# Layernorm and gate of a two-layer network in one block, with the scaling on GpSimd and the spills inside the first attention

## The chip, the cores and the metric

The kernel is written for one Trainium2 chip and runs on 1 of its cores. The metric is the device time of one launch in microseconds (us), shorter is better. Engines are named as the profile names them: PE is TensorE, DVE is VectorE, ACT is ScalarE, POOL is GpSimd, and SP is the sync engine, which issues most of the DMAs.

## The reference

Only the first parts of the first layer touch the change. The input `x` has 8 batches of 512 rows and 256 features.

```python
h = (x - mean(x)) / sqrt(var(x) + 1e-5)          # layernorm over the 256 features
attn = attention(h, W_qkv, W_out)                # 16 key/value heads, 32 query heads, alibi slopes, causal
logits = mean(h, axis=1) @ w_gate + b_gate       # one row of 8 logits a batch
probs = softmax(logits); top_vals, top_idx = top_k(probs, 2)
gate_w = top_vals / sum(top_vals)
a = clip(alpha, 0.1, 1.0)
ffn = a * main(h) + (1 - a) * sum(gate_w[k] * expert[top_idx[k]](h) for k in (0, 1))
x1 = x + silu(ffn) * attn
```

The second layer (a recurrence, a second attention, routing and experts) follows, and the change does not touch it.

## The kernel before

The program is a row of phases. Each opens a block in which every engine has its own instruction stream, and at a block's end all engines meet at a barrier. The first three phases are `layernorm_phase`, `gate_phase` and `head_attention_phase`; then comes `network_phase`, the first reader of the spilled halves and of the gate's results.

`layernorm_phase` makes one pass a batch. SP loads a batch of 512 KB into one of two buffers `x_in`. DVE takes the statistics (`bn_stats`, L113, and `bn_aggr`, L117), ACT the root (L144), and DVE the reciprocal (L119) and the scaling of the batch in place, four instructions of 128x256 (L122). PE transposes it by eight products with the identity (L166) into one of two pairs of PSUM banks. ACT copies each bank into `xh`, rounded to the form in which PE multiplies, and sums the columns into `xsum` (L153). DVE writes the remainder, bank less `xh`, into `xl` (L134). SP stores both halves, 512 KB each, to DRAM (L92, L93).

The loops run over pairs of batches. DVE's order is: all of pass n + 1 up to its scaling, then the remainder of batch n. SP's order is: wait for the transposes of batch n, load batch n + 2, wait for its remainder, store both halves. So a load stands behind the two stores of the batch before it. Loads and passes wrap around: ten loads are issued and DVE and ACT make nine passes, the last of them on a second copy of the first batch, since the loop has no special case for its end. The block ends only when the last store has landed (L96).

`gate_phase` loads the gate's weights, multiplies `xsum` by them on PE (L226), and runs some twelve tiny instructions on DVE, each waiting for the one before (`link`), with one `Exp` on ACT (L232). Beside them GpSimd clears the accumulator `acc` in one instruction (L219). SP then writes two tiny tables to DRAM, `rows` (which expert's weights to load) and `coef` (their factors), waits for both, reads them back in the layout that the network needs (L209 to L213), and waits again before the block ends.

`head_attention_phase` runs 16 heads of 8 batches. SP loads a head's weights (L674, L675, later L696 and L698) and copies each batch's keys `k_parts` within SBUF into two partition halves, `k_twice` (L681). At the start GpSimd splits the first head's weights (L714, L716), and PE's first product waits for that. GpSimd also scales the probabilities in every step (L723).

```python
sp.wait_ge(turned, (pair * 2 + par) + 1)                        # L84
sp.dma_start(x_in[par][:], ...)
sp.wait_ge(low, (pair * 2 + par) + 1)                           # L90
sp.dma_start(xh_dram[...], xh[...]); sp.dma_start(xl_dram[...], xl[...])
```

## Time and profile before

| quantity | value |
|---|---|
| three runs | 3632.81, 3629.51, 3629.32 us |
| their median | 3629.51 us |
| the profiled execution's own time | 3632.09 us |
| its span, first to last instruction | 3630.3 us |
| outside the span (3632.09 less 3630.3) | 1.8 us |
| PE busy over the span | 3332.2 us, 92% |
| DVE, ACT, POOL busy | 68%, 60%, 32% |
| mean granted clock of TensorE | 0.961 |
| from the start to the gate's first instruction | 62.0 us |
| from the gate's first instruction to the attention's first | 13.3 us |
| from the attention's first instruction to PE's first product | 7.9 us |

The profiled execution lies within the three runs, near the slower of them. A share of busy time over the whole span is a mean over stages with different limits: PE is 92% busy in all and almost idle in the first 83 us, which is the stretch that the change rewrites. So the stages are read one by one.

### The profile page before, as it was taken

How to read it: one execution, taken by the hardware profiler on the slowest of the kernel's cores; microseconds unless marked ns; L12 is line 12 of the kernel's file. 1: busy time of each engine (PE TensorE's matmuls, PEld its weight loads, DVE VectorE, ACT ScalarE, POOL GpSimd, SP SyncE). 2: the span in 40 equal slices, each digit the busy share in tenths (PEclk: the TensorE clock that was granted, in tenths of full speed). 3: DMA queues.
4: the chain of work that ended last, by engine and by line, in shares of the span. 5: the costliest groups of instructions: out<-in, count | busy, mean ns of one | idle time of the engine just before them, and what ended most of it. 6: DMA issues, size and time to landing. Idle time of an engine off the chain costs nothing. (4 is left out here: it accounts for less than half of the span.)

```text
span 3630.3 us, 67556 instructions
## 1 busy us (share of the span) xinstructions
PE 3332.2 (92%) x19106; PEld 2540.4 (70%) x19106; DVE 2452.3 (68%) x7032; ACT 2169.8 (60%) x5052; POOL 1178.1 (32%) x1802
## 2 busy tenths in 40 slices
PE   2999999999999999997999997979999965999995
PEld 1777777777777777776888885546666654788885
DVE  5777777777777777776666664546666635666665
ACT  1777777777777777775565554215565640555553
POOL 1333333333333333334333331022313102244442
PEclk9999999999999999999999998978999976999998
DMA  4222222222222222224333432110111123554545
GB/s 163 44 51 45 50 46 47 49 45 51 45 51 45 47 44 49 47 46 154 117 127 127 135 116 96 53 49 22 30 27 30 27 80 110 153 142 122 142 123 156
DMA packets 176586, 281.45 MB, mean 78 GB/s; under 512 B 32466, under 2 KB 118226, under 8 KB 176466
## 3 DMA queue, kind: packets, MB, share of 16 engines
q1 hardware_dynamic: 161874, 259.98, 24.8%
q0 software_dynamic: 14592, 19.93, 3.4%
q8 instruction: 67, 1.10, 0.1%
q14 instruction: 53, 0.43, 0.0%
HBM read 160.84 MB, written 41.16 MB: 56 GB/s over the span
## 5 line engine op out<-in xcount | busy, mean ns | idle before, releaser
L723 POOL TENSOR_SCALAR at_p<-at_p,at_recip 128x128 f32<-128x128 f32 (+3 forms) x1028 | 537.0, 535 | 981.2 <-DVE at_recip L862 981.2
L773 ACT ACTIVATE at_p<-at_p,at_nmax 128x128 f32<-128x128 f32 (+3 forms) x1030 | 575.6, 559 | 291.1 <-DVE at_nmax L856 287.9
L856 DVE CUSTOM_DVE_ANT_0 at_p<-at_s_ps,at_bias 128x128 f32<-128x128 f32 (+3 forms) x1030 | 493.6, 479 | 155.8 <-PE at_s_ps L971 155.8
L978 PE MATMUL at_t_ps<-ident,at_p 128*128 128x128 f32 x2560 | 460.0, 278 | 0.1
L970 PE MATMUL at_s_ps<-at_k_twice,at_q 128*128 128x128 f32 (+3 forms) x1030 | 388.4, 377 | 8.0 <-DVE at_nmax L856 1.2
L1795 DVE CUSTOM_DVE_ANT_0 aa_a_ps<-aa_a_ps,aa_hidden 128x128 f32<-128x128 f32 (+3 forms) x512 | 247.3, 507 | 173.8 <-PE aa_a_ps L1959 170.7
L971 PE MATMUL at_s_ps<-at_k_twice,at_q 128*128 128x128 f32 (+3 forms) x1030 | 332.9, 323 | 0.0
L978 PEld LDWEIGHTS at_t_ps<-ident,at_p 128*128 128x128 f32 x2560 | 294.9, 140 | 46.3 <-DVE at_pT L869 29.9
L988 PE MATMUL at_o_ps<-at_pT,at_v 128*64 128x512 f32 (+3 forms) x2064 | 306.8, 439 | 0.0
L1695 ACT ACTIVATE aa_pT<-aa_b_ps 128x512 f32<-128x512 f32 (+1 forms) x384 | 196.6, 529 | 176.0 <-PE aa_b_ps L1977 173.2
L988 PEld LDWEIGHTS at_o_ps<-at_pT,at_v 128*64 128x64 f32 x2064 | 136.8, 137 | 176.4 <-issue 157.3
L438 ACT ACTIVATE nw_h<-nw_h_ps,nw_b 128x512 f32<-128x512 f32 x192 | 132.2, 689 | 211.8 <-PE nw_h_ps L535 211.4
L970 PEld LDWEIGHTS at_s_ps<-at_k_twice,at_q 128*128 128x128 f32 x1030 | 194.7, 189 | 91.1 <-DVE at_nmax L856 44.6
L869 DVE COPY at_pT<-at_t_ps 128x128 f32<-128x128 f32 (+3 forms) x512 | 238.9, 467 | 0.0
L508 DVE SCALAR_TENSOR_TENSOR nw_hl<-nw_h,nw_coef_now,nw_hh 128x512 fp32r<-128x512 f32 x192 | 154.8, 806 | 115.3 <-ACT nw_hh L443 115.3
L2510 POOL DMA_INDIRECT moe_dram<-ex_o,places x76 | 124.9, 1643 | 302.9 <-ACT ex_o L2537 211.8
L781 ACT ACTIVATE at_pT<-at_t_ps 128x128 f32<-128x128 f32 (+3 forms) x512 | 218.9, 428 | 6.2
L391 POOL TENSOR_SCALAR nw_w1h<-nw_w_raw 128x256 fp32r<-128x256 f32 x200 | 106.7, 533 | 337.5 <-PE nw_o_ps L546 317.2
L843 DVE TENSOR_TENSOR at_k_parts<-at_m_ps,at_k_parts 64x512 fp32r<-64x512 f32 x130 | 88.8, 683 | 179.5 <-ACT at_vT L767 179.5
L1959 PE MATMUL aa_a_ps<-aa_k,aa_q 128*128 128x128 f32 (+3 forms) x512 | 191.3, 386 | 14.8 <-DVE aa_nmax L1795 11.7
L971 PEld LDWEIGHTS at_s_ps<-at_k_twice,at_q 128*128 128x128 f32 x1030 | 196.6, 191 | 11.4
L933 PE MATMUL at_m_ps<-xh,at_wh 128*128 128x512 f32 (+1 forms) x520 | 185.2, 437 | 20.7 <-POOL at_wl L716 18.6
(315 smaller groups left out, 8467.3 us busy)
## 6 DMA issues: line engine op xcount, KB each, us to landing
at_k_twice<-at_k_parts SPq DMA_DIRECT2D x260, 256.0 KB, 3.3
nw_w_raw<-in_w_all_dram SPq DMA_DIRECT2D x52, 1024.0 KB, 7.4
w_raw<-in_w_dram SPq DMA_DIRECT2D x57, 768.0 KB
ln_x<-in_x_dram SPq DMA_DIRECT2D x10, 512.0 KB, 4.8
nw_xh<-xh_dram SPq DMA_DIRECT2D x10, 512.0 KB, 4.4
nw_xl<-xl_dram SPq DMA_DIRECT2D x10, 512.0 KB, 4.9
at_w_raw<-in_w_heads_dram SPq DMA_DIRECT2D x18, 256.0 KB, 3.4
nw_x<-in_x_dram SPq DMA_DIRECT2D x9, 512.0 KB, 7.0
```

The source lines that it names most:

```text
L723: pool.tensor_scalar(p, p, recip[:, u:u + 1], 1.0, ALU.mult, ALU.mult).then_inc(scaled, 1)
L773: act.activation(p_sb[:, u, 0:N], p_sb[:, u, 0:N], ACT.Exp, bias=nmax[:, u:u + 1], scale=-1.0, accum_out=total[:, u:u + 1]).then_inc(exped, 1)
L781: act.activation(pT[par][:, 1, 0:qt + 1, qt * P:N], t_ps[1][:, 0:N].rearrange("p (k q) -> p k q", q=P), ACT.Copy).then_inc(odd_out, 1)
L856: dve.tensor_tensor_reduce(out=p_sb[:, u, 0:N], in0=s_ps[u % 2][:, 0:N], in1=bias[:, u % 2, S - N:S], scale=1.0, scalar=BIG, op0=ALU.add, ...
L869: dve.tensor_copy(pT[par][:, 0, 0:qt + 1, qt * P:N], t_ps[0][:, 0:N].rearrange("p (k q) -> p k q", q=P))\
L970: pe.matmul(s_ps[u % 2][:, 0:N], q, k_twice[par][:, 0, 0:N], start=True, stop=False)
L971: pe.matmul(s_ps[u % 2][:, 0:N], q, k_twice[par][:, 1, 0:N], start=False, stop=True).then_inc(scored, 1)
L978: ins = pe.transpose(t_ps[u % 2][:, k * P:k * P + P], p_sb[:, u, k * P:k * P + P], ident[:])
L988: ins = pe.matmul(o_ps[HD * h:HD * h + HD, k * P:S], v[par][:, k, :], pT[par][:, h, k, k * P:S], start=(k == 0), stop=(k == TT - 1))
L1695: act.activation(pT[group_of(n, s) % 2][:, s % REP, piece * S:piece * S + N], b_ps[done % 3][:, 0:N], ACT.Exp, scale=-1.0)\
L1795: dve.tensor_tensor_reduce(out=a_ps[i % 2][:, 0:N], in0=a_ps[i % 2][:, 0:N], in1=hidden[:, S - N:S], scale=1.0, scalar=BIG, op0=ALU.add, o ...
L1959: pe.matmul(a_ps[i % 2][:, 0:N], q_all[n % 2][:, head // 2, N - P:N], k_all[n % 2][:, head % 2, g, 0:N], start=True, stop=True).then_inc(s ...
```

## The change

There are five edits.

1. The layernorm's loops are written out for 8 batches. There are three buffers `x_in` and three pairs of PSUM banks in place of two, and two sets of `mv` and `rstd`. Exactly eight loads and eight passes are made. DVE's order becomes: reciprocal of n + 1, statistics of n + 2, remainder of n.
2. The scaling is done by GpSimd, four instructions a batch. After each batch's scaling GpSimd clears an eighth of `acc`.
3. The gate is the last part of the layernorm's block, with no barrier ahead of it. Its weights are loaded behind the first three batches. The last remainder stands between its first steps and the rest.
4. The stores of `xh` and `xl` are taken out of the layernorm's block. SP issues one at the end of each head of the attention, `xh` of a batch after an even head and `xl` of it after an odd one: 16 in all.
5. The gate's round trip through DRAM is moved into the attention's SP stream: the writes before the first copies of the keys, the reads after them. The waits for its end and for the stores stand at the end of that block.

POOL, at the start of the program. Before (`ident` is the identity, `acc` the accumulator, `at_rel` the attention's first tile):

```order
L102 AFFINE_SELECT ident<-ident 128x128
L53 UNCONDITIONAL_BRANCH
L217 UNCONDITIONAL_BRANCH
L219 MEMSET acc 128x8192
L181 UNCONDITIONAL_BRANCH
L704 UNCONDITIONAL_BRANCH
```

And with the change:

```order
L116 AFFINE_SELECT ident<-ident 128x128
L122 TENSOR_SCALAR ln_x<-ln_x,ln_mv,ln_rstd 128x256 x4
L124 MEMSET acc 128x2x512
L122 TENSOR_SCALAR ln_x<-ln_x,ln_mv,ln_rstd 128x256 x4
L124 MEMSET acc 128x2x512
L122 TENSOR_SCALAR ln_x<-ln_x,ln_mv,ln_rstd 128x256 x4
```

The pair of rows comes eight times. GpSimd had nothing to do in the layernorm, and now stands between DVE's reciprocal and PE's transposes of every batch; the one long clearing is cut into eight.

DVE, one batch in the middle of the layernorm and the passage into the gate. Before:

```order
L113 BN_STATS ln_stats<-ln_x 128x6 x4
L114 ISA
L115 MEMSET ln_carry 128x1
L117 BN_AGGR ln_mv<-ln_stats 128x2 x4
L118 REGISTER_ALU
L119 RECIPROCAL ln_rstd<-ln_std 128x4
L122 TENSOR_SCALAR ln_x<-ln_x,ln_mv,ln_rstd 128x256 x4
```

With the change, the last batches and the gate's beginning:

```order
L144 RECIPROCAL ln_rstd<-ln_std 128x4
L135 BN_STATS ln_stats<-ln_x 128x6 x4
L140 BN_AGGR ln_mv<-ln_stats 128x2 x4
L150 TENSOR_TENSOR xl<-ln_ps,xh 128x512 x2
L144 RECIPROCAL ln_rstd<-ln_std 128x4
L150 TENSOR_TENSOR xl<-ln_ps,xh 128x512 x2
L172 MEMSET row_sb 8x1
L175 SCALAR_TENSOR_TENSOR gt_logits<-gt_ps,gt_bg 8x8
L177 TENSOR_REDUCE gt_tiny<-gt_logits 8x1
L150 TENSOR_TENSOR xl<-ln_ps,xh 128x512 x2
L180 RECIPROCAL gt_tiny<-gt_tiny 8x1
L181 TENSOR_SCALAR gt_logits<-gt_logits,gt_tiny 8x8
```

The four scalings have left DVE, the reciprocal comes before the next batch's statistics, and the last remainder lies between the gate's second step and its third.

SP, from the attention's start into its loop. Before, the row of `at_k_twice` came right behind that of `at_wo_raw`. With the change:

```order
L648 DMA at_wo_raw<-in_wo_heads_dram 128x256
L657 DMA rows_dram<-row_sb 8x3
L658 DMA coef_dram<-coef_sb 8x3
L654 DMA at_k_twice<-at_k_parts 64x1024 x4
L662 DMA rows<-rows_dram 1x24
L663 DMA coef<-coef_dram 128x24
```

And at the end of an even head:

```order
L673 DMA xh_dram<-xh 256x1x512
L675 ISA
L677 ISA
L677 DMA at_w_raw<-in_w_heads_dram 128x512
L679 ISA
L679 DMA at_wo_raw<-in_wo_heads_dram 128x256
```

The store stands ahead of the loads of a later head's weights, behind all copies of keys of its own head.

The diff without the declarations and without the removed lines, which the listing above shows.

```diff
@@ -48,19 +48,35 @@
...
+    XR = 3
...
+        x_in = [sb(f"ln_x{i}", [P, TT, D]) for i in range(XR)]
...
+        mv = [sb(f"ln_mv{i}", [P, TT, 2]) for i in range(2)]
...
+        rstd = [sb(f"ln_rstd{i}", [P, TT]) for i in range(2)]
...
+        xT_ps = [[ps(f"ln_ps{i}{k}") for k in range(KT)] for i in range(3)]
...
+        x_loaded = [sem(f"ln_x_loaded{i}") for i in range(XR)]
...
@@ -68,32 +84,30 @@
...
         @block.sync
         def _(sp):
...
+            for n in range(B):
+                if n >= XR:
+                    sp.wait_ge(turned, n - XR + 1)
+                sp.dma_start(x_in[n % XR][:], x_view[n]).then_inc(x_loaded[n % XR], 16)
+                if n == XR - 1:
+                    sp.dma_start(wg[:], w_gate.rearrange("(k p) e -> p k e", p=P)).then_inc(loaded, 16)
+                    sp.dma_start(bg[:], b_gate.rearrange("(a e) -> a e", a=1).broadcast_to([B, E0])).then_inc(loaded, 16)
+                    sp.dma_start(al[:], alpha.broadcast_to([B, 1])).then_inc(loaded, 16)
+            sp.wait_ge(loaded, 48)
+            for i in range(XR):
+                sp.wait_ge(x_loaded[i], 16 * len(range(i, B, XR)))
         @block.gpsimd
         def _(pool):
@@ -101,139 +115,42 @@
...
+            for n in range(B):
+                pool.wait_ge(rstd_done, n + 1)
+                for i in range(TT):
+                    pool.tensor_scalar(x_in[n % XR][:, i, :], x_in[n % XR][:, i, :], mv[n % 2][:, i, 0:1],
+                                       rstd[n % 2][:, i:i + 1], ALU.subtract, ALU.mult).then_inc(normed, 1)
+                pool.memset(acc[:, :, n * S:n * S + S], 0.0).then_inc(cleared, 1)
+            pool.wait_ge(cleared, B)
         @block.vector
         def _(dve):
             dve.memset(eps[:], EPS_LN).then_inc(eps_done, 1)
...
+            def spread(n):
+                dve.wait_ge(x_loaded[n % XR], 16 * (n // XR) + 16)
                 for i in range(TT):
...
+                    dve.bn_stats(stats[:, i, :], x_in[n % XR][:, i, :]).then_inc(stats_done, 1)
                 dve.wait_ge(stats_done, n * TT + TT)
...
+                if n >= 2:
+                    dve.wait_ge(normed, (n - 1) * TT)
                 for i in range(TT):
...
+                    dve.bn_aggr(mv[n % 2][:, i, :], stats[:, i, :]).then_inc(var_done, 1)
+            def invert(n):
                 dve.wait_ge(std_done, n + 1)
...
+                dve.reciprocal(rstd[n % 2][:], std[:]).then_inc(rstd_done, 1)
+            def remainder(n):
+                for k in range(KT):
+                    dve.wait_ge(high, n * KT + k + 1)
+                    ins = dve.tensor_tensor(xl[:, k, n * S:n * S + S], xT_ps[n % 3][k][:],
+                                            xh[:, k, n * S:n * S + S].bitcast(F32), ALU.subtract)
+                ins.then_inc(low, 1)
...
@@ -242,11 +159,23 @@
...
+            spread(0)
+            invert(0)
+            spread(1)
+            for n in range(B):
+                if n + 1 < B:
+                    invert(n + 1)
+                if n + 2 < B:
+                    spread(n + 2)
+                if n < B - 1:
+                    remainder(n)
+            dve.memset(row_sb[:, 0:1], 0)
             dve.wait_ge(ready, 1)
             link(dve.scalar_tensor_tensor(out=logits[:], in0=l_ps[0:B, 0:E0], scalar=1.0 / S, in1=bg[:],
                                           op0=ALU.mult, op1=ALU.add))
             link(dve.tensor_reduce(tiny[:, 0:1], logits[:], AX.X, ALU.max, negate=True))
+            remainder(B - 1)
             dve.wait_ge(exped, 1)
             link(dve.reciprocal(tiny[:, 2:3], tiny[:, 1:2]))
             link(dve.tensor_scalar(logits[:], logits[:], tiny[:, 2:3], None, ALU.mult))
@@ -258,8 +187,48 @@
             link(dve.tensor_scalar(coef_sb[:, 0:1], al[:], 0.1, 1.0, ALU.max, ALU.min))
             link(dve.tensor_scalar(tiny[:, 5:6], coef_sb[:, 0:1], -1.0, 1.0, ALU.mult, ALU.add))
             link(dve.tensor_scalar(coef_sb[:, 1:NF], top[:, 0:TOP], tiny[:, 4:5], tiny[:, 5:6], ALU.mult, ALU.mult))
...
             link(dve.tensor_scalar(row_sb[:, 1:NF], at[:, 0:TOP], 1.0, None, ALU.add))
+        @block.scalar
+        def _(act):
+            act.wait_ge(eps_done, 1)
+            def root(n):
+                act.wait_ge(var_done, n * TT + TT)
+                if n >= 1:
+                    act.wait_ge(rstd_done, n)
+                act.activation(std[:], mv[n % 2][:, :, 1], ACT.Sqrt, bias=eps[:, 0:1]).then_inc(std_done, 1)
+            root(0)
+            root(1)
+            for n in range(B):
+                act.wait_ge(turned, n + 1)
+                for k in range(KT):
+                    act.activation(xh[:, k, n * S:n * S + S], xT_ps[n % 3][k][:], ACT.Copy,
+                                   accum_out=xsum[:, k, n:n + 1]).then_inc(high, 1)
+                if n + 2 < B:
+                    root(n + 2)
+            act.wait_ge(chain, 2)
+            act.activation(logits[:], logits[:], ACT.Exp, bias=tiny[:, 0:1], accum_out=tiny[:, 1:2])\
+                .then_inc(exped, 1)
+        @block.tensor
+        def _(pe):
+            pe.wait_ge(id_done, 2)
+            for n in range(B):
+                pe.wait_ge(normed, n * TT + TT)
+                if n >= 3:
+                    pe.wait_ge(low, n - 2)
+                for k in range(KT):
+                    for i in range(TT):
+                        ins = pe.transpose(xT_ps[n % 3][k][:, P * i:P * i + P], x_in[n % XR][:, i, P * k:P * k + P], ident[:])
+                ins.then_inc(turned, 1)
+            pe.wait_ge(loaded, 48)
+            pe.wait_ge(high, B * KT)
+            for k in range(KT):
+                ins = pe.matmul(l_ps[0:B, 0:E0], xsum[:, k, :], wg[:, k, :], start=(k == 0), stop=(k == KT - 1))
+            ins.then_inc(ready, 1)
...
@@ -573,7 +542,8 @@
...
+def head_attention_phase(nc, w_heads, wo_heads, slopes, ident, xh, xl, acc, xh_dram, xl_dram, row_sb, coef_sb,
...
@@ -613,6 +583,9 @@
...
@@ -681,8 +654,14 @@
...
+            sp.dma_start(rows_dram, row_sb[:]).then_inc(gate_out, 16)
+            sp.dma_start(coef_dram, coef_sb[:]).then_inc(gate_out, 16)
             copy_k(1, 0)
             copy_k(4, 1)
+            sp.wait_ge(gate_out, 32)
+            sp.dma_start(rows[:], rows_dram.rearrange("(a b) f -> a (b f)", a=1)).then_inc(gate_back, 16)
+            sp.dma_start(coef[:], coef_dram.rearrange("(a b) f -> a (b f)", a=1).broadcast_to([P, B * NF]))\
+                .then_inc(gate_back, 16)
             with sp.Fori(0, KVH // 2) as jj:
                 for jp in range(2):
                     j = jj * 2 + jp
@@ -690,6 +669,8 @@
                         for par in range(2):
                             copy_k(kv_count(j * B + pair * 2 + (par + 2)), par)
+                    to, half = ((xh_dram, xh), (xl_dram, xl))[jp]
+                    sp.dma_start(to[:, :, ds(jj * S, S)], half[:, :, ds(jj * S, S)].bitcast(F32)).then_inc(spilled, 16)
                     sp.wait_ge(w_split, j + 1)
                     sp.wait_ge(wo_split, j + 1)
@@ -697,6 +678,8 @@
                         .then_inc(w_loaded[jp], 16)
                     sp.dma_start(wo_raw[jp][:], wo_heads[ds((j + 2) % KVH, 1)].rearrange("a p n -> p (a n)"))\
                         .then_inc(w_loaded[jp], 16)
+            sp.wait_ge(gate_back, 32)
+            sp.wait_ge(spilled, 32 * B)
             for i in range(2):
                 sp.wait_ge(w_loaded[i], 32 * (KVH // 2 + 1))
                 sp.wait_ge(k_copied[i], 32 * (KVH * B // 2 + 1))
@@ -2694,14 +2677,16 @@
...
+                layernorm_phase(nc, x, ident, xh, xl, xsum, acc, w_gate, b_gate, alpha, row_sb, coef_sb, spent)
+                head_attention_phase(nc, w_heads, wo_heads, slopes, ident, xh, xl, acc, xh_dram, xl_dram, row_sb, coef_sb,
+                                     rows_dram, coef_dram, rows, coef, spent)
...
                           spent)
...
```

## Rows read from the trace of the kernel before

**Rows 1.** by stage: us; busy PE, PEld, DVE, ACT, POOL; clock, DMA, GB/s

```profile
0.00:62.00 62.00, 15.75 (x64) 12.55 (x64) 39.60 (x143) 13.30 (x42) 0.68 (x6) 1.00 0.66 220
62.00:75.40 13.40, 0.26 (x4) 0.15 (x4) 5.20 (x14) 1.68 (x3) 6.92 (x1) 1.00 0.02 2
...
83.10:100.00 16.90, 13.59 (x42) 9.81 (x42) 5.70 (x19) 6.30 (x17) 0.05 (x1) 0.88 0.29 62
100.00:1600.00 1500.00, 1493.36 (x9106) 1105.23 (x9106) 1181.11 (x3844) 1135.90 (x3078) 561.93 (x1050) 1.00 0.22 47
```

**Rows 2.** timeline, first batch: start, us, engine line op out<-in xcount

```profile
4.71 1.41 DVE L113 BATCH_NORM_STATS2 ln_stats<-ln_x 128x6 f32<-128x256 f32 x4 [3.79 <-DMA ln_x<-in_x_dram]
...
8.24 0.18 DVE L119 RECIPROCAL ln_rstd<-ln_std 128x4 f32<-128x4 f32 x1 [1.71 <-ACT ln_std L144]
...
9.89 1.97 PE L166 MATMUL ln_ps<-ident,ln_x 128*128 128x128 f32 x8 [9.89 <-DVE ln_x L122]
...
11.93 0.18 DVE L119 RECIPROCAL ln_rstd<-ln_std 128x4 f32<-128x4 f32 x1 [0.36 <-ACT ln_std L144]
...
12.60 0.59 ACT L153 ACTIVATE xh<-ln_ps 128x512 f32 x1
...
13.44 1.28 DVE L134 TENSOR_TENSOR xl<-ln_ps,xh 128x512 f32 x2
```

**Rows 3.** timeline, statistics of the third batch and of the ninth pass

```profile
15.78 1.40 DVE L113 BATCH_NORM_STATS2 ln_stats<-ln_x 128x6 f32<-128x256 f32 x4 [1.05 <-DMA ln_x<-in_x_dram]
...
51.80 1.41 DVE L113 BATCH_NORM_STATS2 ln_stats<-ln_x 128x6 f32<-128x256 f32 x4 [1.09 <-DMA ln_x<-in_x_dram]
```

**Rows 4.** timeline, the gate and the boundaries around it

```profile
62.03 6.92 POOL L219 MEMSET acc<- 128x8192 f32 x1 [60.52 <-POOLq L53]
...
64.75 0.15 DVE L249 TENSOR_REDUCE gt_tiny<-gt_logits 8x1 f32<-8x8 f32 x1
...
65.62 3.35 DVE L252 TENSOR_SCALAR gt_logits<-gt_logits,gt_tiny 8x8 f32<-8x8 f32 x1
...
70.50 0.15 DVE L262 TENSOR_SCALAR gt_row<-gt_at 8x2 uint32<-8x2 uint32 x1
...
75.53 0.58 DVE L818 CAST at_woh<-acc 128x256 fp32r<-128x256 f32 x1 [4.89 <-PEq L181]
```

**Rows 5.** POOL: one timeline row of the attention scaling; one group

```profile
1208.36 0.94 POOL L723 TENSOR_SCALAR at_p<-at_p,at_recip 128x256 f32<-128x256 f32 x2 [1.22 <-DVE at_recip L862]
...
L716 POOL TENSOR_TENSOR at_wol<-at_wo_raw,at_woh 128x256 fp32r<-128x256 f32 x16 | 11.8, 735 | 1.3
```

**Rows 6.** DMA issues: out<-in, engine, op, count, KB each, us to landing

```profile
at_k_twice<-at_k_parts SPq DMA_DIRECT2D x260, 256.0 KB, 3.3
...
ln_x<-in_x_dram SPq DMA_DIRECT2D x10, 512.0 KB, 4.8
...
xl_dram<-xl SPq DMA_DIRECT2D x8, 512.0 KB, 4.1
```

**Rows 7.** timeline of SP at the end of the first head

```profile
196.56 0.35 SPq L696 DMA_DIRECT2D at_w_raw<-in_w_heads_dram  x1
...
207.07 86.35 SPq L681 DMA_DIRECT2D at_k_twice<-at_k_parts  x16
```

**Rows 8.** timeline, a copy of k issued and the first read of it

```profile
1205.82 13.30 SPq L681 DMA_DIRECT2D at_k_twice<-at_k_parts  x4
...
1213.44 0.32 PE L970 MATMUL at_s_ps<-at_k_twice,at_q 128*128 128x128 f32 x1
```

**Rows 9.** waits of SP and timeline at the end of the attention

```profile
SPq L585 <- PEq L585: 8.3, 1, 8.3
...
1670.41 0.06 DVE L452 MEMSET nw_bsum<- 128x4 f32 x1 [0.36 <-PEq L585]
```

**Rows 10.** timeline, two of the first products of the attention, on PE

```profile
84.15 1.05 PE L933 MATMUL at_m_ps<-xh,at_wl 128*128 128x512 f32 x2
...
91.90 0.63 PE L933 MATMUL at_m_ps<-xh,at_wl 128*128 128x512 f32 x2
```

More of the change, by code:

```diff
@@ L73, in layernorm_phase @@
         low = sem("ln_low")
-        spilled = sem("ln_spilled")
+        loaded = sem("gt_loaded")
+        chain = sem("gt_chain")
+        exped = sem("gt_exped")
+        ready = sem("gt_ready")
         x_view = x_dram.rearrange("b (i p) d -> b p i d", p=P)
@@ L125, in _ @@
-            norm(0, 0, 0)
-            with dve.Fori(0, B // 2) as pair:
-                for par in range(2):
-                    n = pair * 2 + par
-                    norm(n + 1, pair + par, 1 - par)
-                    dve.wait_ge(high, n * KT + KT)
-                    at = n * S
-                    for k in range(KT):
-                        ins = dve.tensor_tensor(xl[:, k, ds(at, S)], xT_ps[par][k][:], xh[:, k, ds(at, S)].bitcast(F32),
-                                                ALU.subtract)
-                    ins.then_inc(low, 1)
@@ L138, in _ @@
-        @block.scalar
-        def _(act):
-            act.wait_ge(eps_done, 1)
-            def root(n):
-                act.wait_ge(var_done, n * TT + TT)
-                act.activation(std[:], mv[:, :, 1], ACT.Sqrt, bias=eps[:, 0:1]).then_inc(std_done, 1)
-            root(0)
-            with act.Fori(0, B // 2) as pair:
-                for par in range(2):
-                    n = pair * 2 + par
-                    root(n + 1)
-                    act.wait_ge(turned, n + 1)
-                    for k in range(KT):
-                        act.activation(xh[:, k, ds(n * S, S)], xT_ps[par][k][:], ACT.Copy,
-                                       accum_out=xsum[:, k, ds(n, 1)]).then_inc(high, 1)
@@ L156, in _ @@
-        @block.tensor
-        def _(pe):
-            pe.wait_ge(id_done, 2)
-            with pe.Fori(0, B // 2) as pair:
-                for par in range(2):
-                    n = pair * 2 + par
-                    pe.wait_ge(normed, n * TT + TT)
-                    for k in range(KT):
-                        for i in range(TT):
-                            ins = pe.transpose(xT_ps[par][k][:, P * i:P * i + P], x_in[par][:, i, P * k:P * k + P], ident[:])
-                    ins.then_inc(turned, 1)
@@ L573, in _ @@
             turn(B, 1)
-def head_attention_phase(nc, w_heads, wo_heads, slopes, ident, xh, xl, acc, spent):
+def head_attention_phase(nc, w_heads, wo_heads, slopes, ident, xh, xl, acc, xh_dram, xl_dram, row_sb, coef_sb,
+                         rows_dram, coef_dram, rows, coef, spent):
     with ExitStack() as ctx:
```

115 lines of the change are left out of this document (21 added, 94 removed).

## The prediction, made before the change was run

> **What bounds the kernel now.** I read the times by stage first [rows 1]. In the attention, from 100 to 1600 us, PE is busy for 1493.4 of 1500 us: nothing that leaves PE's work there alone can shorten it. In the first 62 us PE is busy for 15.8 us, and in the 13.4 us of the gate for 0.3. So the start is bound by chains of waits and the rest by PE. The change touches only the start, and moves some DMAs under the attention.
>
> Then the timeline of the layernorm [rows 2, 3]. The statistics of the third batch begin at 15.78 and those of the ninth pass at 51.80: six passes in 36.0 us, 6.0 a pass, and each waits about 1 us for the DMA of its batch. DMA runs at 220 GB/s there [rows 1]: a pass moves 1.5 MB, a load behind two stores, and the load lands 4.8 us after its issue in the median [rows 6]. After the ninth pass come the last stores, and the gate begins at 62.03.
>
> Last the gate [rows 4]. DVE's tiny instructions take 0.15 us each, save one of 3.35 us, which ends at 68.97, where GpSimd's clearing of `acc` ends too (62.03 plus 6.92 is 68.95). The nine after it end at 70.65, 0.19 each. Then comes the round trip through DRAM, and DVE's first instruction of the attention stands at 75.53, after 4.89 us of idle time.
>
> **The change, part by part.** All is measured up to that last point, DVE's first cast of the attention.
>
> *First batch.* The statistics begin at 4.71 as before and the reciprocal ends at 8.42 [rows 2]. Scaling is now GpSimd's. The trace has no such instruction (two scalars a row) on GpSimd; the nearest is the scaling of the probabilities, same size, one such scalar, two in 0.94 us, 0.47 each [rows 5]. The other end is GpSimd's instruction with two whole inputs of that size, 0.735 [rows 5]. I take 0.47, since only one tensor is read: 1.88 us a batch, against 1.4 on DVE. With the hand-offs the transposes start at 10.5 and, at 1.97 us [rows 2], end at 12.5.
>
> *Each further batch.* Three costs compete. DVE: statistics and their sum 1.82 (4.71 to 6.53, where the 1.71 us of idle time before the reciprocal begins), reciprocal 0.18, remainders 1.28 [rows 2], with gaps 3.5. GpSimd: 1.88 of scaling plus an eighth of 6.92 [rows 4], 0.87, so 2.75. One of three buffers round its loop: load 3.9 (DVE waited 3.79 us for the first), statistics 1.82, root and reciprocal 0.54 [rows 2], scaling 1.88, transposes 1.97, hand-offs 0.3: 10.4, a third of it 3.5. The first and the last are equal, and as DVE works in a fixed order each delays the other at times. Placing the eight batches one after another with these durations, each engine in its written order, I get the last transposes ending at 38.7: 26.2 us for seven batches, 3.75 each in place of 6.0. ACT's two copies, 0.59 each and a read of the sum behind each [rows 2], end at 40.1. The stores are no longer there to be waited for, and neither is the ninth pass. Against 62.0 that is 21.9 us less.
>
> *Gate.* Its weights landed long before. The product takes 0.3 with its hand-off (0.26 busy [rows 1]), DVE's first two steps 0.4, then the last remainder 1.28, which covers ACT's table load and `Exp`, then eleven steps at 0.19, 2.1: it ends at 44.2. The 3.35 us stall goes, as GpSimd's last clearing ends near 38. The round trip, most of the 4.89 us, leaves the path: the writes and reads are tiny and have the whole attention to land. A barrier costs 0.36 us where nothing else is late [rows 9]. DVE's first cast then stands at 44.6 instead of 75.53, 30.9 less. I take 30.5, for hand-offs that I cannot price.
>
> That stall is where the Trainium skill bears on this change. Taken by itself, the row says that a DVE instruction can stand still as long as a GpSimd instruction runs; were that so for the statistics, DVE's 3.5 and GpSimd's 2.75 would add, and that is a rival below. The Trainium skill (SBUF — State Buffer, "Who interferes with whom") says that the two share a pair of ports, an exclusive lock, which a DVE instruction wants only in a two-port mode or with two inputs in SBUF. By it neither the statistics (one input) nor the remainder (one input in PSUM) waits, and the time would be 3599.0 us, as below, and not the 3616.5 of the first reading. No row of this trace has the statistics beside GpSimd, so the row does not settle it.
>
> *Attention.* Its first 8 us are unchanged. Sixteen stores of 512 KB are added, 8.4 MB. Each is issued behind the copies of keys of its head. At a head's end the weights' load is issued at 196.56 and the next copy of keys at 207.07 [rows 7]; a store lands within 4.1 us [rows 6]. So it is gone before the next copy. A copy has cover of its own: issued at 1205.82, its second half 0.6 later, landing 3.3 us after that, and first read at 1213.44 [rows 8], 3.7 us to spare. The first weights are needed a head later. The gate's four DMAs stand where SP has nothing to issue but the next keys. I cost all of it at nothing; if the cover were gone it would be the 4.1 us of a store, sixteen times. At the end SP waited 8.3 us for the others at the barrier [rows 9]; the last store takes at most 0.6 plus 4.1 of that.
>
> **Sum.** 3632.1 less 30.5 is 3601.6 against the profiled execution. That execution lies 2.6 us above the median of the three runs; against the median I get **3599.0 us**.
>
> Bounds: with transposes at 1.2 us a batch (PE has two levels of speed, below) and a load in 3.3, the same placing gives 3.5 less. With GpSimd at 0.735 and loads at 4.8 it gives 5.6 more. The runs before spread over 3.5 us.
>
> **The rivals.**
>
> *A. GpSimd and DVE take turns* (8 in 100). For it: the row of 3.35 us. Against it: the reduction at 64.75, beside the same clearing, took its usual 0.15 [rows 4]. A batch would take 3.5 plus 2.75, 6.25 us, so 2.5 more for seven batches: 17.5 us, 3616.5 us.
>
> *B. PE reaches its upper level earlier* (8 in 100). In the first products of the attention a pair took 1.05 us at 84.15 and 0.63 at 91.90 [rows 10]; I read that as the lower level, 1.2 GHz, and the upper, 2.4 GHz, though the granted clock is 0.88 in the mean over that stretch [rows 1]. PE had been almost idle since the layernorm's last transposes. With the change it rests some 14 us between those, at 38.7, and its first product at 52.5. Six pairs came before the row at the upper level; were they at that level, each would save 0.42 us at most, and three more later if the clock held: nine pairs, 3.8 us, 3595.2 us.
>
> *C. The stores reach PE, and the kernel is slower* (3 in 100). The place is `k_twice`: SP's queue is served in order, so a store that still moves data when the next copy is issued delays it; PE has nothing else to do, being 99.6% busy. Each store would have to cost PE more than 30.5 over 16, 1.9 us, for a loss. If its full 4.1 us came through at each head it would be 65.6 us: 3664.6 us. Against it stand the 10.5 us between head's end and next copy.
>
> *D. The gain is given back* (3 in 100). The waits moved to the attention's end would have to end last there, beyond the 8.3 us of SP's waiting, or the layernorm's pass would have to stay at 6 us because of its loads. With both, the time would be within 7 us of the one before: 3627.
>
> **How the numbers follow.** My forecast has 78 in 100, and is the likeliest. The range goes from 3593 (3599.0 less the 3.5 of the lower bound and part of B's 3.8) to 3608 (the upper bound, 3604.6, and the spread of the runs). It holds the forecast and B, and leaves out A, C and D, 14 in 100, and some of the forecast's own error. A measurement of this kernel can tell 0.2%, 7.3 us, from no change. Faster by more than that are the forecast, A and B: 0.94. Within it is D: 0.03. Slower is C: 0.03.
>
> **What would show it right or wrong.** Right: GpSimd's scalings near 0.47 us each, statistics starting 3.5 to 4 us apart, DVE's statistics still 1.41 us for four, no DVE instruction of some us in the gate, DVE's first cast near 44.6, PE as busy in the attention as before, and no wait of PE for `k_twice`. Wrong: a scaling of 0.7 us or more, statistics stretched wherever GpSimd works (A), loads that land later than 4.8 us though no store is there, a row of PE waiting for the copies (C), or SP as the last engine at the attention's end (D).

## The result and the profile of the changed kernel

| | before | changed kernel |
|---|---|---|
| median of 7 runs, us | 3629.68 (3627.29 to 3633.75) | 3617.72 (3610.81 to 3620.19) |
| ratio, 95% interval | | 0.9961 (0.9951 to 0.9971) |
| profiled execution, us (its span) | 3632.09 (3630.3) | 3613.86 (3612.1) |
| mean granted clock | 0.961 | 0.962 |
| DVE's first cast of the attention, us | 75.53 | 61.41 |

The changed kernel is 0.39% faster: by the ratio 14.2 us of 3629.7, with an interval from 10.5 to 17.8; the two medians differ by 12.0. The forecast said 30.5 us and 3599.0 us, with a range up to 3608; the result lies 9.7 us above that range. The first cast of the attention moved by 14.12 us, which lies within the interval of the gain. So the search is for the 16.8 us that are missing ahead of one instruction (61.41 where 44.6 was forecast); the median is 18.7 us above the forecast, and the other 1.9 us are taken up at the end of the section on why the prediction was wrong.

First the page and the table by stage (start and end, length, then busy PE, PEld, DVE, ACT, POOL, granted clock, DMA share, GB/s), which answers to [rows 1].

```profile
PE 3329.0 (92%) x19106; PEld 2537.6 (70%) x19106; DVE 2434.8 (67%) x6978; ACT 2168.2 (60%) x5051; POOL 1212.5 (34%) x1841
```

```profile
0.00:56.70 56.70, 15.72 (x64) 12.55 (x64) 24.00 (x88) 13.17 (x42) 46.29 (x46) 1.00 0.23 74
56.70:61.20 4.50, 0.25 (x4) 0.17 (x4) 3.26 (x15) 1.61 (x3) 0.00 (x0) 1.00 0.00 0
69.00:100.00 31.00, 27.10 (x130) 19.33 (x132) 17.36 (x57) 18.51 (x49) 8.01 (x16) 0.94 0.25 52
100.00:1600.00 1500.00, 1493.36 (x9110) 1104.77 (x9106) 1181.37 (x3845) 1134.86 (x3077) 556.13 (x1044) 1.00 0.24 52
```

Three things stand there. The layernorm has lost its stores and its ninth pass: DMA runs at 74 GB/s where it ran at 220. DVE has lost 15.6 of 39.6 us. And GpSimd, idle there before, is busy for 46.29 of 56.70 us, more than any other engine. In the attention PE is as busy as before, to the hundredth.

The timeline shows what the layernorm now waits for (start, duration, engine, line, operation, operands, count, and in brackets the idle time before it with what ended it).

```profile
4.75 1.41 DVE L135 BATCH_NORM_STATS2 ln_stats<-ln_x 128x6 f32<-128x256 f32 x4 [3.83 <-DMA ln_x<-in_x_dram]
8.58 4.84 POOL L122 TENSOR_SCALAR ln_x<-ln_x,ln_mv,ln_rstd 128x256 f32<-128x256 f32 x4 [7.05 <-DVE ln_rstd L144]
13.37 0.94 POOL L124 MEMSET acc<- 128x1024 f32 x1
14.30 4.82 POOL L122 TENSOR_SCALAR ln_x<-ln_x,ln_mv,ln_rstd 128x256 f32<-128x256 f32 x4
19.07 0.94 POOL L124 MEMSET acc<- 128x1024 f32 x1
20.00 4.81 POOL L122 TENSOR_SCALAR ln_x<-ln_x,ln_mv,ln_rstd 128x256 f32<-128x256 f32 x4
24.95 1.41 DVE L135 BATCH_NORM_STATS2 ln_stats<-ln_x 128x6 f32<-128x256 f32 x4 [1.68 <-DMA ln_x<-in_x_dram]
30.57 1.97 PE L225 MATMUL ln_ps<-ident,ln_x 128*128 128x128 f32 x8 [3.73 <-POOL ln_x L122]
53.35 1.97 PE L225 MATMUL ln_ps<-ident,ln_x 128*128 128x128 f32 x8 [3.73 <-POOL ln_x L122]
57.42 1.29 DVE L150 TENSOR_TENSOR xl<-ln_ps,xh 128x512 fp32r<-128x512 f32 x2
58.80 0.22 DVE L181 TENSOR_SCALAR gt_logits<-gt_logits,gt_tiny 8x8 f32<-8x8 f32 x1
60.53 0.16 DVE L190 TENSOR_SCALAR row_sb<-gt_at 8x2 uint32<-8x2 uint32 x1
61.41 0.51 DVE L801 CAST at_woh<-acc 128x256 fp32r<-128x256 f32 x1 [0.72 <-PEq L62]
...
68.95 1.20 PE L916 MATMUL at_m_ps<-xh,at_wh 128*128 128x512 f32 x2 [11.94 <-POOL at_wl L699]
69.94 1.06 PE L916 MATMUL at_m_ps<-xh,at_wl 128*128 128x512 f32 x2
...
73.07 0.63 PE L916 MATMUL at_m_ps<-xl,at_wh 128*128 128x512 f32 x2
```

GpSimd's rows follow each other without idle time: four scalings in 4.82 us, a piece of the clearing, four scalings. A pass is 5.70 us (8.58, 14.30, 20.00), PE waits 3.73 us for GpSimd in each, and eight passes end with the transposes at 55.3. DVE's waits of 1.6 to 1.8 us for a load come from the same cause, since a buffer is loaded again only when its transposes are done. The grouped rows give the price of one scaling in the last columns (busy us, mean ns of one):

```profile
L122 POOL TENSOR_SCALAR ln_x<-ln_x,ln_mv,ln_rstd 128x256 f32<-128x256 f32 x32 | 38.5, 1209 | 7.1 <-DVE ln_rstd L144 7.0
```

It is 1.21 us, where the forecast took 0.47 and gave 0.735 as its upper end [rows 5].

The DMAs: first the rows of SP around the end of the first head, then those of the issues (count, KB each, median us to landing).

```profile
178.76 1.10 SPq L654 DMA_DIRECT2D at_k_twice<-at_k_parts  x2
180.21 0.72 SPq L673 DMA_DIRECT2D xh_dram<-xh  x1
181.36 0.59 SPq L677 DMA_DIRECT2D at_w_raw<-in_w_heads_dram  x1
...
190.94 1.16 SPq L654 DMA_DIRECT2D at_k_twice<-at_k_parts  x2
```

```profile
at_k_twice<-at_k_parts SPq DMA_DIRECT2D x260, 256.0 KB, 3.7
...
xh_dram<-xh SPq DMA_DIRECT2D x8, 512.0 KB, 4.9
xl_dram<-xl SPq DMA_DIRECT2D x8, 512.0 KB, 5.0
```

```profile
SPq L555 <- PEq L555: 4.7, 1, 4.7
```

The store is issued 10.7 us ahead of the next copy and lands in 4.9. No wait of PE for `k_twice` is listed in the attention. At its end SP still waits 4.7 us for PE, 8.3 before [rows 9]: the last store is not what ends it.

### The profile page after: what moved, and what is told of

Same layout as the page of the kernel before. It is cut to its first block and busy times, and to the rows that moved or that the text cites. A ratio compares the mean times of both kernels' runs of the same rounds, so it can differ in the third digit from the quotient of the medians.

```text
span 3612.1 us, 67403 instructions
## 1 busy us (share of the span) xinstructions
PE 3329.0 (92%) x19106; PEld 2537.6 (70%) x19106; DVE 2434.8 (67%) x6978; ACT 2168.2 (60%) x5051; POOL 1212.5 (34%) x1841
## 5 line engine op out<-in xcount | busy, mean ns | idle before, releaser
L953 PEld LDWEIGHTS at_s_ps<-at_k_twice,at_q 128*128 128x128 f32 x1030 | 194.3, 189 | 91.0 <-DVE at_nmax L839 44.6
```

What stands on the lines that cost most here:

```text
L953: pe.matmul(s_ps[u % 2][:, 0:N], q, k_twice[par][:, 0, 0:N], start=True, stop=False)
```

## The experiments

Eleven kernels ran. Each is the changed kernel with the edit shown, or with an edit on top of an earlier one where the text says so; only the one with the stores alone is the kernel before with an edit. The cast in the text below is always DVE's first cast of the attention.

**What makes GpSimd's scaling dear.** Three readings were open: the operation, a subtraction; the second scalar that is read for each row; or the work of other engines beside it. The first three kernels change the operations and the scalars alone, and the same number of such instructions runs in the same places. None of the three computes the layernorm: the first leaves out the mean, the second the multiplication by the reciprocal, and the third multiplies by the reciprocal twice and leaves out the mean.

```diff
-                    pool.tensor_scalar(x_in[n % XR][:, i, :], x_in[n % XR][:, i, :], mv[n % 2][:, i, 0:1],
-                                       rstd[n % 2][:, i:i + 1], ALU.subtract, ALU.mult).then_inc(normed, 1)
+                    pool.tensor_scalar(x_in[n % XR][:, i, :], x_in[n % XR][:, i, :], rstd[n % 2][:, i:i + 1],
+                                       1.0, ALU.mult, ALU.mult).then_inc(normed, 1)
```

> GpSimd's scaling of a 128x256 tile took 1.20 us in the changed kernel, four in 4.82, where I had taken 0.47 from the attention's scaling. Here it multiplies by the reciprocal (one scalar a row) and by the constant 1.0, as the attention's does; the subtraction of the mean is left out. Theory S (the second scalar a row is what costs): 0.47 each, four in 1.9. Theory O (the operation subtract costs): also 0.47. Theory D (the tile, its DMA, or DVE's work beside it costs): 1.20 as before. By S or O the layernorm runs as I had forecast, DVE's first cast of the attention near 45 instead of 61.4; by D it stays at 61.4.

The second keeps the subtraction, and multiplies by a constant:

```diff
-                                       rstd[n % 2][:, i:i + 1], ALU.subtract, ALU.mult).then_inc(normed, 1)
+                                       1.0, ALU.subtract, ALU.mult).then_inc(normed, 1)
```

> GpSimd subtracts the mean (one scalar a row) and multiplies by the constant 1.0; the scaling by the reciprocal is left out. Theory S (two scalars a row): 0.47 us a tile, first cast near 45. Theory O (subtract): 1.20, first cast at 61.4. Theory D (tile or neighbours): 1.20 and 61.4.

The third reads two scalars and multiplies by both:

```diff
-                    pool.tensor_scalar(x_in[n % XR][:, i, :], x_in[n % XR][:, i, :], mv[n % 2][:, i, 0:1],
-                                       rstd[n % 2][:, i:i + 1], ALU.subtract, ALU.mult).then_inc(normed, 1)
+                    pool.tensor_scalar(x_in[n % XR][:, i, :], x_in[n % XR][:, i, :], rstd[n % 2][:, i:i + 1],
+                                       rstd[n % 2][:, i:i + 1], ALU.mult, ALU.mult).then_inc(normed, 1)
```

> GpSimd multiplies twice by the reciprocal, two scalars a row, no subtract; the mean stays in. Theory S (two scalars a row): 1.20 us a tile, first cast at 61.4. Theory O (subtract): 0.47 and near 45. Theory D: 1.20 and 61.4.

The group of the scaling in each of the three, in the order above:

```profile
L122 POOL TENSOR_SCALAR ln_x<-ln_x,ln_rstd 128x256 f32<-128x256 f32 x32 | 14.7, 476 | 12.9 <-DVE ln_rstd L144 12.9
```

```profile
L122 POOL TENSOR_SCALAR ln_x<-ln_x,ln_mv 128x256 f32<-128x256 f32 x32 | 36.0, 1134 | 7.0 <-DVE ln_rstd L144 7.0
```

```profile
L122 POOL TENSOR_SCALAR ln_x<-ln_x,ln_rstd 128x256 f32<-128x256 f32 x32 | 17.3, 552 | 11.6 <-DVE ln_rstd L144 11.6
```

One scalar with a multiplication takes 476 ns, one scalar with a subtraction 1134, two scalars with two multiplications 552. The second scalar as the cause wanted the third dear and the second cheap, and both came out the other way. The work of others beside it wanted all three dear. What is left is the operation, O: a subtraction in this instruction, the one with scalars (`tensor_scalar`). The casts stand at 43.47, 58.81 and 44.67, and the single runs took 3598.03, 3616.49 and 3601.36 us. With the scaling at the price that the forecast had taken (the first), the cast is 1.1 us ahead of the forecast's 44.6.

The trace of the changed kernel limits this to that instruction. With two whole inputs (`tensor_tensor`), GpSimd's subtraction (L699) takes the time of a multiplication (L1646) and of an addition (L1649):

```profile
L699 POOL TENSOR_TENSOR at_wl<-at_w_raw,at_wh 128x512 fp32r<-128x512 f32 x17 | 21.8, 1282 | 1.4
L1646 POOL TENSOR_TENSOR aa_turn<-aa_turn,aa_rope 128x512 f32<-128x512 f32 x16 | 20.4, 1277 | 21.2 <-DMA aa_turn<-aa_turn 20.1
L1649 POOL TENSOR_TENSOR aa_turn<-aa_turn 128x512 f32<-128x512 f32 x16 | 20.4, 1275 | 1.3
```

So the row of 735 ns [rows 5], the forecast's upper end, was itself a subtraction, and gave no warning.

**Whether a place or a sign helps.** If a subtraction is dear and an addition not, the layernorm can be written x * rstd + shift, with shift = -mean * rstd, which DVE makes for a batch in one instruction of 0.16 us. The clearing stands ahead of the scalings in this kernel, as in the next two.

```diff
+                dve.wait_ge(rstd_done, n + 1)
+                dve.scalar_tensor_tensor(out=shift[n % 2][:], in0=mv[n % 2][:, :, 0], scalar=-1.0, in1=rstd[n % 2][:],
+                                         op0=ALU.mult, op1=ALU.mult).then_inc(shifted, 1)
...
-                    pool.tensor_scalar(x_in[n % XR][:, i, :], x_in[n % XR][:, i, :], mv[n % 2][:, i, 0:1],
-                                       rstd[n % 2][:, i:i + 1], ALU.subtract, ALU.mult).then_inc(normed, 1)
+                    pool.tensor_scalar(x_in[n % XR][:, i, :], x_in[n % XR][:, i, :], rstd[n % 2][:, i:i + 1],
+                                       shift[n % 2][:, i:i + 1], ALU.mult, ALU.add).then_inc(normed, 1)
```

> The same layernorm, with GpSimd multiplying by the reciprocal and adding a shift, minus the mean times the reciprocal, which DVE makes in one more tiny instruction a batch; acc is cleared first. GpSimd took 1.20 us a tile for subtract and multiply, 1.13 for a subtract with one scalar, 0.54 for two multiplies. Theory O1 (subtract alone is slow on GpSimd): 0.54 a tile, no longer the longest, first cast of the attention near 45 as with two multiplies (44.7), total 16 us below the changed kernel, about 3601. Theory O2 (anything that is not a multiply is slow, add too): 1.1 to 1.2 a tile, first cast at 55.5, total 3611. The pass is then set by the buffers' loop.

Its group, and its waits of DVE for loads (us in total, times, the longest):

```profile
L126 POOL TENSOR_SCALAR ln_x<-ln_x,ln_rstd,ln_shift 128x256 f32<-128x256 f32 x32 | 17.3, 554 | 11.2 <-DVE ln_shift L149 11.1
```

```profile
DVE ln_stats L138 <- DMA ln_x<-in_x_dram: 7.0, 4, 3.8
```

554 ns; the cast stands at 45.31 and the median is 3602.09 us, a ratio to the kernel before of 0.992 (0.9906 to 0.9934). GpSimd is idle 11.2 us before its scalings, so it is no longer the bound.

The same with the sign of shift turned (scalar=1.0) and a subtraction as the second operation tells whether it is the subtraction or its place ahead of the multiplication:

```diff
-                                       shift[n % 2][:, i:i + 1], ALU.mult, ALU.add).then_inc(normed, 1)
+                                       shift[n % 2][:, i:i + 1], ALU.mult, ALU.subtract).then_inc(normed, 1)
```

> As the kernel with multiply and add, but the shift has the other sign and GpSimd multiplies and then subtracts it: the same result by subtract in the second place. Theory O1 (subtract is slow on GpSimd wherever it stands): about 1.1 to 1.2 us a tile and first cast near 55.4. Rival P (it is slow only as the first operation, or the pair multiply and add is the fast one): 0.54 and 45.3, the place tells.

```profile
L126 POOL TENSOR_SCALAR ln_x<-ln_x,ln_rstd,ln_shift 128x256 f32<-128x256 f32 x32 | 38.5, 1210 | 0.1
```

1210 ns again, the cast at 55.39, 3612.12 us in one run. So the subtraction is dear in either place. These two kernels compute the same layernorm with the same instructions beside them and differ only in the second operation and the sign of shift.

**The clearing in GpSimd's loop.** The eight pieces stand ahead of the first scaling, where GpSimd waited 7 us for the first batch:

```diff
             for n in range(B):
+                pool.memset(acc[:, :, n * S:n * S + S], 0.0).then_inc(cleared, 1)
+            for n in range(B):
...
-                pool.memset(acc[:, :, n * S:n * S + S], 0.0).then_inc(cleared, 1)
```

> GpSimd clears acc in eight pieces ahead of its first scaling, while the first batch is on its way, and not behind each scaling. If GpSimd's own work sets the pass (4.82 plus 0.94 makes the 5.70 seen), the pass falls to 4.85 us: the last scaling ends at 8.6 plus 8 times 4.85, 47.4, the last transposes at 49.5, and the first cast comes near 55.4, 6 us earlier than 61.4; in the runs 6 us less than the changed kernel, about 3611. If the loads or DVE's order set the pass, it stays at 5.7 and the first cast at 61.4. If the clearing does not fit into the 7 us before the first reciprocal, up to 0.7 us of the gain is lost.

Two rows of its timeline of GpSimd:

```profile
1.48 7.19 POOL L119 MEMSET acc<- 128x1024 f32 x8
8.68 12.05 POOL L124 TENSOR_SCALAR ln_x<-ln_x,ln_mv,ln_rstd 128x256 f32<-128x256 f32 x10
```

The cast moves from 61.41 to 55.29, 6.1 us, for seven pieces of 0.87 (an eighth of 6.92 [rows 4]; the row of 0.94 overlaps its neighbours). The median is 3611.99 us, a ratio of 0.995 (0.9936 to 0.9964). Ten scalings run without a gap, so GpSimd is still the bound. Against this kernel the one with the addition has its cast at 45.31: the dear operation is worth 10.0 us of what remains.

**What each other part is worth.** The scaling back on DVE, behind the reciprocal, with the clearing first:

```diff
-                    pool.tensor_scalar(x_in[n % XR][:, i, :], x_in[n % XR][:, i, :], mv[n % 2][:, i, 0:1],
-                                       rstd[n % 2][:, i:i + 1], ALU.subtract, ALU.mult).then_inc(normed, 1)
...
+                dve.wait_ge(rstd_done, n + 1)
+                for i in range(TT):
+                    dve.tensor_scalar(x_in[n % XR][:, i, :], x_in[n % XR][:, i, :], mv[n % 2][:, i, 0:1],
+                                      rstd[n % 2][:, i:i + 1], ALU.subtract, ALU.mult).then_inc(normed, 1)
```

> The changed kernel with the scaling on DVE again, right behind the reciprocal, and acc cleared by GpSimd first. DVE then has 3.5 plus 1.4 a pass, 4.9 us: less than GpSimd's 5.70. I expect the last scaling to end near 43.5, the gate near 51 and the first cast near 52, 9 us earlier than 61.4, total about 3608. If the scaling had to leave DVE for the gain, the first cast would come at 61 or later.

```profile
22.27 1.40 DVE L130 BATCH_NORM_STATS2 ln_stats<-ln_x 128x6 f32<-128x256 f32 x4
26.66 1.40 DVE L130 BATCH_NORM_STATS2 ln_stats<-ln_x 128x6 f32<-128x256 f32 x4
```

```profile
L142 DVE TENSOR_SCALAR ln_x<-ln_x,ln_mv,ln_rstd 128x256 f32<-128x256 f32 x32 | 11.0, 407 | 0.3
```

The statistics come 4.4 us apart and the cast stands at 48.07, earlier than the 52 that was expected: a pass took 4.4 us where 4.9 had been allowed. The median is 3605.08 us, a ratio of 0.9928 (0.9914 to 0.9942). On DVE the same subtraction and multiplication costs 0.34 us (11.0 us for 32; one alone lasts 407 ns in the mean, and neighbours overlap). So the move to GpSimd as the change makes it, clearing included, costs 13.3 us (61.41 less 48.07) against leaving the scaling where it was.

Both stores back in the layernorm, each batch's behind the load as in the kernel before, the rest as changed:

```diff
+                if n >= XR:
+                    spill(n - XR)
+            for n in range(B - XR, B):
+                spill(n)
+            sp.wait_ge(ln_spilled, 32 * B)
...
-                    to, half = ((xh_dram, xh), (xl_dram, xl))[jp]
-                    sp.dma_start(to[:, :, ds(jj * S, S)], half[:, :, ds(jj * S, S)].bitcast(F32)).then_inc(spilled, 16)
```

> The changed kernel with both stores of a batch back in the layernorm's block, each pair behind the load that comes after its batch, and the block's end waiting for them. My theory: GpSimd's 5.70 us a pass sets the layernorm, so the stores cost only their tail: the last pair, issued at 58.8, lands near 63.5, and the first cast comes at about 64, 2.6 us later than 61.4. Rival: the loads are late behind the stores, as before the change, and the pass goes to 6.0 or more: first cast at 66 to 67. If the stores' move was the main gain, the first cast would be beyond 70. The attention itself as long as in the changed kernel, 1593 us from its first cast to the next block.

```profile
63.80 0.50 DVE L808 CAST at_woh<-acc 128x256 fp32r<-128x256 f32 x1 [3.13 <-PEq L62]
```

The cast moves by 2.4 us, and the bracket says where: DVE is idle for 3.13 us at the block's end instead of 0.72, while the last stores land. The pass stays at 5.70, and DVE's waits for loads at 12.5 us in all, 12.6 in the changed kernel: behind GpSimd the loads have time. The median is 3619.46 us, a ratio of 0.9966 (0.9952 to 0.9979).

The gate in a block of its own, with the load of its weights and the round trip inside (the diff shows what leaves the layernorm; the same lines stand in the gate's own block):

```diff
-            sp.wait_ge(loaded, 48)
...
-            dve.wait_ge(ready, 1)
...
-            link(dve.scalar_tensor_tensor(out=logits[:], in0=l_ps[0:B, 0:E0], scalar=1.0 / S, in1=bg[:],
-                                          op0=ALU.mult, op1=ALU.add))
```

> The changed kernel with the gate in a block of its own, its weights loaded there, and its round trip through DRAM inside it; acc is still cleared in the layernorm. From the rows of before: a barrier 0.4, the weights' load 2.2, the round trip and its waits 4.9 less the plain boundary 0.7: 6.8 us later, first cast at 68.2, total about 3623. If it is under 3 us, the gate's place was worth little and the gain lies in the layernorm's passes.

```profile
68.05 0.51 DVE L829 CAST at_woh<-acc 128x256 fp32r<-128x256 f32 x1 [4.91 <-PEq L186]
```

The cast stands at 68.05, where 68.2 was expected. The 4.91 us before it, against 0.72, are the round trip on the path again, 4.2 of the 6.6 us; the other 2.4 are the gate's own boundary and load. The median of 11 runs is 3623.97 us, a ratio of 0.9983 (0.9974 to 0.9992).

**The stores alone, in the kernel before.** This one is the kernel before with nothing but both stores moved into the attention; its ninth pass, its gate and DVE's scaling stay:

```diff
-                    sp.wait_ge(low, (pair * 2 + par) + 1)
-                    sp.wait_ge(high, (pair * 2 + par) * KT + KT)
-                    at = (pair * 2 + par) * S
-                    sp.dma_start(xh_dram[:, :, ds(at, S)], xh[:, :, ds(at, S)].bitcast(F32)).then_inc(spilled, 16)
-                    sp.dma_start(xl_dram[:, :, ds(at, S)], xl[:, :, ds(at, S)].bitcast(F32)).then_inc(spilled, 16)
...
-            sp.wait_ge(spilled, 32 * B)
...
+                    to, half = ((xh_dram, xh), (xl_dram, xl))[jp]
+                    sp.dma_start(to[:, :, ds(jj * S, S)], half[:, :, ds(jj * S, S)].bitcast(F32)).then_inc(spilled, 16)
```

> The kernel before with edit 4 alone: its two-buffer loops, nine passes, scaling on DVE and the gate apart stay, only the stores are moved into the attention. In the changed kernel they were worth 2.4 us, under GpSimd's 5.7 us passes. My theory: in the kernel before they held the loads, so here the pass falls from 6.0 to DVE's and the loads' 5.0 to 5.3, eight times 0.7 to 1.0, and the tail of 4 us goes: first cast at 64 to 66 in place of 75.5, total about 3620. Rival: the pass was not held by the stores, only the tail goes: 71.5, total 3626.

```profile
15.69 1.41 DVE L106 BATCH_NORM_STATS2 ln_stats<-ln_x 128x6 f32<-128x256 f32 x4 [1.03 <-DMA ln_x<-in_x_dram]
...
45.35 1.39 DVE L106 BATCH_NORM_STATS2 ln_stats<-ln_x 128x6 f32<-128x256 f32 x4
50.79 6.92 POOL L212 MEMSET acc<- 128x8192 f32 x1 [49.28 <-POOLq L53]
54.47 3.27 DVE L245 TENSOR_SCALAR gt_logits<-gt_logits,gt_tiny 8x8 f32<-8x8 f32 x1
64.47 0.58 DVE L815 CAST at_woh<-acc 128x256 fp32r<-128x256 f32 x1 [5.06 <-PEq L174]
```

From the third batch's statistics to the ninth pass's there are now 29.7 us, 36.0 before [rows 3]: 4.9 a pass in place of 6.0, with no wait for a load behind the third batch. A load lands in 3.8 us in the median, 4.8 before [rows 6]. The clearing at the gate's start, at 62.03 before [rows 4], stands 11.2 us earlier: 6.4 by the passes and 4.8 by the last stores, which no longer hold the block. The cast moves 11.1 us, and the median is 3619.02 us, a ratio of 0.9969 (0.9957 to 0.9981). This one part gives nearly the gain of the whole change; by the medians it is 12.5 us against 12.0, with 6.9 to 15.6 by its interval, so the runs alone don't part the two. In the changed kernel it is worth 2.4 us only: the passes' share is hidden there behind GpSimd.

**A version that beats both.** The addition, the clearing first, and a fourth input buffer against the waits that were left to DVE:

```diff
-    XR = 3
+    XR = 4
```

> Multiply and add on GpSimd, acc cleared first, and now four buffers for x in place of three. In the kernel with three, DVE waited 3.2 us for loads beyond the first. If the buffers' loop still held the passes, that wait goes and the first cast moves from 45.3 to 42 or 43, total 2 to 3 us less, about 3599.5. If DVE's own 3.6 us a pass hold them, the cast moves by under 1 us.

```profile
DVE ln_stats L138 <- DMA ln_x<-in_x_dram: 3.8, 1, 3.8
```

```profile
21.64 1.40 DVE L138 BATCH_NORM_STATS2 ln_stats<-ln_x 128x6 f32<-128x256 f32 x4
25.06 1.40 DVE L138 BATCH_NORM_STATS2 ln_stats<-ln_x 128x6 f32<-128x256 f32 x4
28.25 1.40 DVE L138 BATCH_NORM_STATS2 ln_stats<-ln_x 128x6 f32<-128x256 f32 x4
42.14 0.50 DVE L807 CAST at_woh<-acc 128x256 fp32r<-128x256 f32 x1 [0.72 <-PEq L62]
```

Only the first load is waited for, a pass takes 3.2 to 3.4 us, DVE's own work, and the cast stands at 42.14. The median is 3596.38 us, a ratio of 0.9908 (0.9893 to 0.9924): 35 us less than the kernel before in the same rounds, and by the medians 21 less than the changed one.

## Why the prediction was wrong

The sign and the place were right, the size was not. By the steps of the prediction:

- **The step that failed** is in the first batch: "I take 0.47, since only one tensor is read: 1.88 us a batch". The four instructions took 4.82 us. The upper end, 0.735, was too low as well: both ends were chosen by the number of inputs, and the price hung on the operation within this instruction. The row behind 0.47 [rows 5] is a multiplication by one scalar and a constant; the row behind 0.735 is a subtraction, but of two whole inputs, where it costs no more than an addition. The new instruction subtracts a scalar first. With a multiplication and an addition, two scalars read, it took 554 ns; a subtraction in either place made it 1134 to 1210.
- **Each further batch.** Three costs were set against each other, DVE 3.5, the buffer's loop 3.5, GpSimd 2.75. The method holds with the right term: GpSimd's is 4.82 plus 0.87, 5.69, and the pass measured 5.70. Eight scalings and seven pieces of clearing from 8.58 on end at 53.3, and the transposes at 55.3. At the forecast's price (476 ns, the first experiment) the cast stood at 43.47: from the changed kernel's 61.41 that is 17.9 us for this one term. The rest of the forecast placed the cast 1.1 us too late, and the two make the 16.8 that were missing. That the third experiment, at 552 ns, stood at 44.67, within 0.1 us of the forecast, is in part luck: a dearer scaling met a placing that was too slow.
- **The clearing at nothing beside it** was right only while GpSimd had time to spare. With GpSimd as the bound its seven pieces cost the 6.1 us that the experiment gave back.
- **The stores.** In the changed kernel they were worth 2.4 us, in the kernel before 11.1. The forecast put their wait and the ninth pass into one sum of 21.9, which could not show that the first is hidden as soon as another engine is slower than the loads.
- **The gate.** The tail from the end of ACT's last copy and read of its sum (56.6) to the cast (61.41) is 4.8 us; 4.5 was forecast (40.1 to 44.6). The difference is the boundary: DVE idles 0.72 us there, where 0.36 was taken. The stall of 3.35 us is a row of 0.22 now, and no GpSimd work runs beside it. Apart again, the gate costs 6.6.
- **The attention at no cost** held: PE is busy for 1493.36 of 1500 us, as before. The copies' median landing rose from 3.3 us [rows 6] to 3.7 and used up cover, no time. The stores did not raise it: it is 3.6 with both stores back in the layernorm, and 3.3 with the stores alone in the attention. What did is open.
- **Rival A**, whose 3616.5 us is nearly the measured time, did not happen: DVE's four statistics take 1.37 to 1.41 us beside GpSimd's work and 1.41 before it, and GpSimd's take 4.81 to 4.84 whatever DVE does. That agrees with the rule quoted from the Trainium skill (SBUF — State Buffer, "Who interferes with whom"). Its time was met by another mechanism.
- **Rival B** happened in small part. PE's first products begin at 68.95, and the row of 0.63 us, the upper level, stands at 73.07, 3.1 us behind the row of 1.06 at 69.94; before, it stood 7.8 us behind the row of 1.05 [rows 10]. But PE fell back to 1.06 us at 77.43 after a wait of 2.00 for DVE. From the cast to the next block the kernel took 1593.0 us where it took 1594.9, and not even that can be put down to the earlier rise: the kernel with the stores alone, whose first six pairs all take 1.05 us or more like those before, took 1593.1, and the one with four buffers, whose pairs take 0.62 to 0.75 from the fourth to the twelfth, took 1595.6. **C** did not show at all. Of **D** the words on a pass that stays near 6 us came true, but by GpSimd and not by the loads.

The parts add up as follows. By the cast's place the change gives 14.1 us: 6.6 by the gate's place and 2.4 by the stores, each measured by undoing it alone; both undone together was not run, so that they add is taken, not shown. The other 5.1 are what is left of the ninth pass's removal, the third buffer, the loops written out and the end of the 3.35 us stall, after the 13.3 us that GpSimd's scaling with its clearing takes back. The stall belongs here: with the gate apart again, but `acc` cleared before it, the same row took 0.22 us too. These parts were not measured one by one.

The medians don't follow the casts exactly: from the kernel before, the changed kernel's median moved by 2.2 us less than its cast, that of the five timed kernels with three buffers by 0.9 to 2.7 less, and that of the stores alone and of the four buffers by 1.4 and 1.7 more. The runs of one kernel spread over 2.6 to 9.4 us. The profiled executions show where such a difference can come from: of the 18.2 us between the two spans, 14.1 lie ahead of the cast, 1.9 between the cast and the next block, and 2.2 behind it, in code that is the same. Over all thirteen profiled executions that last part, the same code in each, took 1955.8 to 1960.8 us, and the part from the cast to it 1593.0 to 1595.6. So some us of any median's difference come from behind the cast. Why these parts vary stays open.

## What to carry to other kernels

When work moves to another engine, price it by a row of that engine with the same instruction and the same operation, not by one that shares the shape, or the operation alone: on GpSimd a `tensor_scalar` with a subtraction took twice the time of one with an addition, while a `tensor_tensor` subtraction took no more than an addition. Rewriting x minus mean as a multiplication and an addition gave 10 us. Where no such row exists, the range must reach as far as the sum hangs on it, and here it hung on it 32 times. And what a part is worth depends on the bound around it: undo each part in the changed kernel and do it alone in the kernel before; the two numbers for the stores, 2.4 and 11.1 us, tell which engine hides the rest.

## What the runs showed of the hardware

- GpSimd, one input of 128x256 f32 with scalars of a row: 476 ns for a multiplication (the second scalar a constant), 552 for two multiplications, 554 for a multiplication and an addition, 1134 for a subtraction and a constant, 1209 and 1210 for a subtraction before or behind a multiplication. Why the subtraction is dear no run tells. DVE did the same subtraction and multiplication at one every 344 ns, 407 ns in the mean for one.
- GpSimd, two whole inputs of 128x512 f32: 1282 ns for a subtraction, 1277 for a multiplication, 1275 for an addition; of 128x256, 737 for a subtraction. There the subtraction is not dear.
- DVE's statistics (one input) and its remainders (one input in PSUM) ran beside GpSimd's scalings at their usual 1.4 and 1.3 us.
- DVE's tiny scaling in the gate took 3.35 us beside GpSimd's clearing [rows 4], 3.27 beside it in the kernel with the stores alone, and 0.22 with GpSimd idle. Its neighbours beside the same clearing took 0.15.
